# Second cross attention of a two-layer decoder: score products in four quarters of the array, two banks used once, and a new order of steps

## The reference, cut to what matters

```
q = (x @ W_q).reshape(b, n, 8, 64); k, v the same from the context
sim = einsum('bihd,bjhd->bhij', q, k) * 64**-0.5
sim = where(mask, sim, -max)
out = einsum('bhij,bjhd->bihd', softmax(sim), v) @ W_o + b_o
```

## Time and profile before

| | |
|---|---|
| time, median of 3 runs | 274.4 us |
| the three runs | 270.34, 274.4, 275.8 us |
| profiled execution, first to last instruction (span) | 267.4 us |
| TensorE busy | 251.2 us, 94% |
| VectorE, ScalarE, GpSimd busy | 186.4, 146.3, 83.7 us |

### The profile page before, as it was taken

The page is one execution under the profiler, slowest core; times in us unless marked ns, Lnnn a source line. Parts: engine busy times, 40 slices in busy tenths (PEclk is TensorE's granted clock), DMA queues, the critical chain, the costliest instruction groups (busy, mean ns, idle before and its releaser), DMA issues.

```text
span 267.4 us, 5236 instructions
## 1 busy us (share of the span) xinstructions
PE 251.2 (94%) x1842; PEld 174.3 (65%) x1842; DVE 186.4 (70%) x628; ACT 146.3 (55%) x303; POOL 83.7 (31%) x139
## 2 busy tenths in 40 slices
PE   8999899999898999999999768899998999999995
PEld 8663588867665656766675423667986566777775
DVE  4458696799765846476324997668566588889975
ACT  0566665552655587787756335464735944443550
POOL 7733994001010446456765131083331000000000
PEclk9999999999999999999999997999999999999999
DMA  5799900033711000000000000000000000000002
GB/s 143 156 311 251 270 16 2 0 78 101 215 29 53 1 0 0 2 1 0 2 1 1 0 2 0 2 0 2 5 5 0 0 0 4 0 0 2 0 1 81
DMA packets 21991, 11.64 MB, mean 44 GB/s; under 512 B 10968, under 2 KB 20957, under 8 KB 21965
## 3 DMA queue, kind: packets, MB, share of 16 engines
q1 hardware_dynamic: 20925, 10.94, 15.0%
q0 software_dynamic: 80, 0.20, 0.7%
q10 hardware_dynamic: 960, 0.16, 0.3%
HBM read 8.68 MB, written 2.62 MB: 42 GB/s over the span
## 4 chain that ended last, share of the span: by engine, by line
PE 76%; DVE 9%; DMA 5%; ACT 4%; issue 3%; POOL 1%; POOLq 0%; SPq 0%; DVEq 0%
PE bank L1007 10%; PE bank L995 9%; PE bank L884 6%; PE bank L865 5%; PE bank L859 5%; PE bank L764 4%; PE bank L921 3%; PE bank L942 3%; PE bank L743 3%; PE bank L632 3%; PE bank L642 2%; DMA v_scratch<-QKVT 2%; PE bank L667 2%; PE bank L750 2%; PE bank L902 2%
## 5 line engine op out<-in xcount | busy, mean ns | idle before, releaser
L514 POOL TENSOR_TENSOR X<-X,att 128x128 f32<-128x128 f32 x72 | 30.1, 454 | 20.0 <-ACT att L1439 20.0
L440 POOL TENSOR_TENSOR rs<-rs,halves 128x4 f32<-128x4 f32 x14 | 14.3, 1020 | 69.0 <-DVE rs L1696 65.8
L995 PE MATMUL bank<-XT,Wb 128*128 128x512 f32 x64 | 30.0, 600 | 0.7 <-ACT XT L1293 0.7
L1007 PE MATMUL bank<-Wb,att 128*128 128x128 f32 x224 | 27.1, 277 | 0.0
L1007 PEld LDWEIGHTS bank<-Wb,att 128*128 128x128 f32 x224 | 26.1, 192 | 1.4 <-issue 1.4
L1479 ACT ACTIVATE att<-bank 128x512 f32<-128x512 f32 x32 | 18.7, 599 | 8.7 <-PE bank L995 8.5
L1439 ACT ACTIVATE att<-bank,comb 128x128 f32<-128x128 f32 x72 | 20.2, 379 | 4.1 <-PE bank L884 4.1
L1873 DVE SCALAR_TENSOR_TENSOR att<-bank,cols,att 128x512 f32<-128x512 f32 x18 | 13.5, 750 | 11.7 <-ACT att L1428 6.6
L884 PEld LDWEIGHTS bank<-W2a,att 128*128 128x128 f32 x144 | 17.9, 192 | 4.1 <-issue 2.9
L884 PE MATMUL bank<-W2a,att 128*128 128x128 f32 x144 | 18.7, 276 | 0.0
L865 PE MATMUL bank<-XT,W3a 128*128 128x512 f32 x36 | 18.1, 598 | 0.3 <-DVE att L1873 0.3
(11 more groups left out here) (230 smaller groups left out, 513.6 us busy)
## 6 DMA issues: line engine op xcount, KB each, us to landing
Wb<-in_L_ffn_W SPq DMA_DIRECT2D x1, 1024.0 KB, 5.2
Wb<-in_L_ffn_W SPq DMA_DIRECT2D x8, 128.0 KB, 4.8
X<-in_x SPq DMA_DIRECT2D x2, 256.0 KB, 3.2
k_scratch<-QKVT SPq DMA_DIRECT2D x1, 512.0 KB, 3.1
q_scratch<-QKVT SPq DMA_DIRECT2D x1, 512.0 KB, 2.8
Wb<-k_scratch SPq DMA_DIRECT2D x1, 512.0 KB, 4.5
v_scratch<-QKVT SPq DMA_DIRECT2D x1, 512.0 KB, 5.4
V<-q_scratch SPq DMA_DIRECT2D x1, 512.0 KB, 6.2
```

Source lines behind the costliest of these rows:

```text
L440: nc.gpsimd.tensor_tensor(rs[:, 0, cut], rs[:, 1, cut], halves[:, :], ALU.pow).then_inc(l_root[h], 1)
L514: nc.gpsimd.tensor_tensor(X[:, h * HT + t, :], X[:, h * HT + t, :], part0[:, i % 2, t, :], ALU.add).then_inc(f_acc, 1)
L995: mm(bank[i % 4][:, :], W1b[:, e, f * P:(f + 1) * P], XT[:, half(h)], start=True, stop=True).then_inc(m_up, 1)
L1007: last = mm(bank[4 + h][:, t * P:(t + 1) * P], hid[:, e % 2, f, tile], W2b[:, e, f, :], start=(f == 0), stop=(f == F1 - 1))
```

## The change

- `scores1(t)` puts a tile's two batches in two banks, `bank[0]` and `bank[1]`, 256 columns each, for every tile. The rows of the array still come from `h2`, the columns now from `o = h2 ^ b2`: the products go round four quarters, (0,0), (1,1), (0,1), (1,0). There are two mask products of 256 columns for one of 512. Each tile now waits for the subtraction of the tile before (`c_sub >= t`), no longer of the one before that.
- banks 0 and 1 become one tensor, so that `subtract_max1` can read both in one instruction; it orders its output as before. `weigh_values1` picks the transposed probabilities from where `o` put them.
- `add_states` has four steps for five, with the same instructions.
- the lists of steps on all engines get a new order, and some steps a wait that the new order needs (`values0`, `up0_first`, `transpose_xn`, `search_bits`).

```diff
-        bank = [ctx.enter_context(nc.psum_tensor(f"bank{i}", [P, 512], fp32)) for i in range(8)]
+        bank01 = ctx.enter_context(nc.psum_tensor("bank01", [P, 2, 512], fp32))
+        bank = [bank01[:, i, :] for i in range(2)]
+        bank += [ctx.enter_context(nc.psum_tensor(f"bank{i}", [P, 512], fp32)) for i in range(2, 8)]
...
(transpose_xn)
+                if n == 3 and h == 1:
+                    pe.wait_ge(s_gelu[0], 1)
+                if n == 4 and h == 0:
+                    pe.wait_ge(kv_ready, 11)
(values0)
+                pe.wait_ge(ld_x0, 80)
+                pe.wait_ge(prep_act, 2 + h)
(scores1)
-                if t >= 2:
-                    pe.wait_ge(c_sub, t - 1)
-                dst = bank[t % 2]
-                bias = per_col(maskrow[0:1, t * P:(t + 1) * P], NHP)
-                mm(dst[:, :], onesb[0:1, :], bias, start=True, stop=False, skip_group_check=True)
+                if t >= 1:
+                    pe.wait_ge(c_sub, t)
+                for b2 in range(2):
+                    bias = per_col(maskrow[0:1, t * P + b2 * S:t * P + (b2 + 1) * S], NHP)
+                    mm(bank[b2][:, 0:NHP * S], onesb[0:1, :], bias, start=True, stop=False, skip_group_check=True)
                 for hp in range(NHP):
                     for b2 in range(2):
                         for h2 in range(2):
-                            tok = slice(t * P + b2 * S, t * P + (b2 + 1) * S)
-                            last = mm(dst[h2 * S:(h2 + 1) * S, (2 * hp + b2) * S:(2 * hp + b2 + 1) * S],
+                            tok, o = slice(t * P + b2 * S, t * P + (b2 + 1) * S), h2 ^ b2
+                            last = mm(bank[b2][o * S:(o + 1) * S, hp * S:(hp + 1) * S],
                                       Q1T[h2 * DH1:(h2 + 1) * DH1, hp, tok], K1T[h2 * DH1:(h2 + 1) * DH1, hp, tok],
(weigh_values1)
-                                      PTs[b2 * S:(b2 + 1) * S, t % 2, hp * P + h2 * S:hp * P + (h2 + 1) * S],
+                                      PTs[b2 * S:(b2 + 1) * S, t % 2, hp * P + o * S:hp * P + (o + 1) * S],
(subtract_max1)
-                s = bank[t % 2][:, :].rearrange("p (a s) -> p a s", s=S)
-                then(V.tensor_reduce(sm[:, t, 0, :], s, AX.X, ALU.max))
+                s = bank01[:, :, 0:NHP * S].rearrange("p b (a s) -> p a b s", s=S)
+                peak = sm[:, t, 0, :].rearrange("p (a b) -> p a b", b=2)
+                then(V.tensor_reduce(peak, s, AX.X, ALU.max))
(search_bits)
+                dve.wait_ge(c_pv, NT - 1)
```

More of the change, by code:

```diff
@@ L579, in _ @@
             add_part(1, 2, 1)
+            root(3, 0)
             add_part(1, 2, 2)
@@ L1068, in _ @@
             scores(3)
+            transpose_probs(0)
             transpose_values(0)
@@ L1071, in _ @@
             transpose_values(2)
-            transpose_probs(0)
-            scores(4)
             transpose_probs(1)
             transpose_values(3)
+            weigh_values(0)
+            scores(4)
+            transpose_probs(2)
             scores(5)
             scores(6)
-            transpose_probs(2)
-            weigh_values(0)
             power(1)
+            transpose_probs(3)
             weigh_values(1)
-            transpose_probs(3)
             weigh_values(2)
@@ L1085, in _ @@
             power(2)
+            weigh_values(3)
+            transpose_probs(5)
+            power(3)
             scores(7)
-            weigh_values(3)
-            power(3)
-            transpose_probs(5)
+            power(4)
             weigh_values(4)
+            scores(8)
             transpose_probs(6)
-            power(4)
-            scores(8)
             weigh_values(5)
@@ L1239, in _ @@
             transpose_probs1(2)
+            scores1(5)
             weigh_values1(1)
-            scores1(5)
             project_out(0)
+            transpose_probs1(3)
             scores1(6)
-            transpose_probs1(3)
             weigh_values1(2)
@@ L1561, in _ @@
             cross0_q(1)
+            weigh0(0, 1)
             silu(0, 4)
@@ L1655, in _ @@
             gelu(0, 1, 1)
+            copy_ys(0, 0)
             for e in range(E1):
@@ L2124, in _ @@
             add_states(0, 3)
-            add_states(0, 4)
             ln_moments(4, 0)
             states_moments(1)
+            states_scale(1)
             ln_apply(4, 0)
-            states_scale(1)
             states_apply(1)
@@ L2165, in _ @@
             ln_apply(5, 1)
-            search_bits()
             route()
```

116 lines of the change are left out of this document (57 added, 59 removed).

## The result

The changed kernel takes 279.14 us in the median of 4 runs (274.53 to 282.0); the kernel before took 272.37 in its 4 runs beside them. The ratio is 1.0225, with a 95% interval from 1.0141 to 1.0308: slower, by 1.4 to 3.1%. The ratios and intervals of this text take only the runs that lie within 1.5% of the fastest of the same kernel, while its medians and its means of lost time take all of them, so the two can differ. The forecast was 274.0 us and a range up to 277.0. It was wrong, and on the slow side.

What follows compares the result with a forecast made beforehand. TensorE, busy 251.2 of 267.4 us, was taken to bound the kernel, with VectorE setting the pace in two places. Terms -1.4 + 0 + 1.0 + 0 = -0.4 gave span 267.0 and time 274.0 us, range 269.5 to 277.0.

Steps and rivals of the forecast that it cites:

- The step that failed: Before the second cross attention's first scores: the clock fall at 160 to 164 us comes again, 1.6 us lost.
- The sum: All terms: -1.4 second cross attention, 0 at 26 us, +1.0 first attention, 0 for the rest; -0.4 us in all.
- Rival B: At 167 to 171 us: clock falls a second time if the wait before scores1(1) reaches 1.4; 276.0 us, chance 0.14.
- my own other wait of a microsecond, at 72 us: First attention: transpose_probs(15), already waiting 0.78 us at 72.25 for copy_probs(14), goes to 73.25.
- The products in four quarters: Second cross attention's score products: 0.62 us a tile for 1.08, so 0.46 gained each, 3.7 us for eight tiles.
- Rival C: Score products: placing doesn't matter, passes stay at 34 ns while the second bank is gone; 277.2 us, chance 0.09.
- Single buffering and the opening: Second cross attention: waits of 1.4 before scores1(1), 0.85 before scores1(5); opening 0.35 late, net gain taken as 1.4 us.
- The 1.75 "given back to waits": Opening of the second cross attention: loss to waits that double buffering hid, against 1.4 us won in three tiles.
- The gap at 26 us: First attention: wait before scores(2) goes, TensorE idles 1.7 before weigh_values(0); between -1.45 and +0.3, taken as 0.
- The gap at 64 us: First attention: subtract_max(14) behind ln_apply(1, 0) leaves VectorE idle 1.2 us, later steps late; +1.0, bounds 0 and +1.4.
- The 274.4: Starting time of the kernel before, median of three runs, 7.0 us above its profiled span of 267.4.

Runs made afterwards that it cites:

- e8: The kernel before, unchanged, run for a second profile: 270.51 us.
- e18: Repeat of e17 (e1 with 6 unused products before scores1(1) and 1 before scores1(2)): 271.75 us, ratio 1.0079.
- e3: Changed kernel with the score products in two quarters of the array again, two banks and single buffering kept: 281.5 us, ratio 1.0432.
- e12: Kernel before with the new lists of steps up to 70 us alone: 276.66 us.
- e16: e12 with 5 unused products right before transpose_probs(15): 272.01 us, ratio 1.0074.
- e4: Changed kernel with subtract_max(14) back ahead of ln_apply(1, 0) on VectorE: 277.04 us, ratio 1.0263.
- e15: e14 with 22 unused products in TensorE's waits: 265.74 us, ratio 0.9835 to the kernel before.
- e14: Kernel before up to 165 us, then the change's score products and order, second tile's scores in banks 3 and 4: 268.55 us, ratio 0.9943.
- e7: Changed kernel with 67 unused products in TensorE's waits: 276.0 us, ratio 1.0203 to the kernel before.
- e11: Changed kernel with 30 unused products, at the same places as e7: 270.57 us, ratio 1.0043 to the kernel before.
- e1: Kernel before with the change's score part alone (four quarters, two banks, single buffered), all lists in the old order: 277.8 us, ratio 1.0208.
- e17: e1 with 6 unused products right before scores1(1) and 1 before scores1(2): 273.92 us, ratio 1.0103 to the kernel before.
- the two halves of the change: Kernel before with the score part alone in the old order: 277.8 us; changed kernel's order alone, with the score part of before: 277.98 us.
- e10: Changed kernel with the second tile's scores in banks 3 and 4: 276.72 us, ratio 1.0217 to the kernel before.

## Why the prediction was wrong

**The step that failed** is the one on the clock: "the same thinness is there after the change, so I expect the fall again: 1.6 us lost". One fall, at the place and of the size that the profile of before happened to have, was carried over, and every other wait was priced at its own length. That fall did not even come: in the profile of the changed kernel the granted clock is 1.00 from 160 to 173, and the way from the transposes of the fourth normalisation to scores1(0), forecast at 7.9 us with a fall in it, is 6.75 us (167.21 to 173.96) against 8.44 before (158.39 to 166.83). Falls came at 26, 77 and 176 instead. The sum has no term for a change in what the clock takes, and measured it is 6.9 us (10.3 lost against 3.4). The page of before could have warned: the runs there spread over 5.5 us while the profiled one had a single fall of 1.6. I called that scatter; e8 and the 81 runs show that it is mostly the clock.

**Rival B** named the mechanism and the place: "it decides if the wait before scores1(1) is 1.4 us or more". The wait was 1.75, the clock fell at 176.6, and e18 shows, for the old order, that filling such a wait takes the fall away. It was sized at one fall of 1.7; it was two such, 3.4 us in this profile, and it had a chance of 0.14 for want of a second look at my own other wait of a microsecond, at 72 us. The argument "against", that 148 to 154 was as thin and the clock held, is no argument: in e8 the fall came at 154 to 158, right behind it.

**The products in four quarters:** right. 0.62 us a tile measured, and e3 shows that the placing does it. Rival C is out. (Its size didn't follow from its own terms either: a gain of 1.4 without the 3.7 is a loss of 2.3, not 1.4 to 2.2.) In the changed kernel the placing is worth 2.2 us of the 3.7 at full clock (e3 against it); that waits for the subtraction take the rest is likely, but was not measured.

**Single buffering and the opening:** the waits were sized nearly right, 1.75 and 0.95 for 1.4 and 0.85. From scores1(0) to the transposes of the fifth normalisation the changed kernel takes 35.0 us (173.96 to 208.95) and the kernel before 33.7 (166.83 to 200.57), but 3.4 of the 35.0 are clock, so at full clock the part is 2.1 us shorter. The forecast has 1.7 for this: its start 0.6 late and its end 1.1 early. (The 1.75 "given back to waits" hold that late start; the waits in the opening were 1.15 of it.) What was priced too low is the way there: from the transposes of the second normalisation (80.34, after: 87.48) to those of the fourth (158.39, after: 167.21) the changed kernel takes 79.7 us and the one before 78.05, of which the forecast had 1.2 for ln_apply(4, 0) behind states_scale(1). The other 0.5 was not followed up. And by the transposes of the second normalisation the changed kernel is 7.1 us late: 5.1 of these are the two falls, 1.0 was forecast, and most of the rest is the late load of Q that follows here.

**The gap at 26 us:** the trade was as laid out, and its wait, forecast at 1.7, is 1.69 or 1.70 in eight of the nine profiles with the new early order. In the profile shown it is 1.20, and two things stand ahead of it there. The load of Q from DRAM landed later, which has no part in the change, and the copy that widens Q held TensorE for 2.19 us; then came the fall at 26. In e12 the load was as late (7.6 us in both), TensorE waited 2.40 us, the clock held, and the wait is 1.69: so it is the slow clock that ate into the wait, and a wait of 2.40 us can pass without a fall.

**The gap at 64 us:** forecast +1.0. VectorE's idle time is as forecast (1.23 for 1.2). From the transposes of the first normalisation to the second, e16, in which the clock held there, takes 15.05 us (66.37 to 81.42) against 14.32 before (66.02 to 80.34): 0.7, its unused products lying inside the wait. e4, which undoes the step, agrees as far as its runs can tell (0.9). Its larger price was behind it: the 0.38 us that it added to the wait before transpose_probs(15) makes a fall there likely (five profiles of five, against two of eight), and filling that wait is worth 4.7 us (e12 against e16).

**The sum.** At full clock the changed kernel is 1.1 us slower than before, forecast -0.4. That error of 1.5 would have stayed inside the range. The 6.9 of the clock did not. The starting point was off too, and hid part of the miss. The distance of 7.0 us between span and median isn't a property of the kernel: every run lists a span 1.7 to 1.8 us below its time, and the rest is longer spans. The 274.4 came from three runs, two of them high, of a kernel whose median over 81 runs is 270.4. From there the same sum gives 270.0, 9 us below the measured 279.14 and not 5.

## What to carry to other kernels

Before pricing a new order, run the old kernel several times and work out span x clock and span x (1 - clock) of each: if the second scatters, the kernel sits at the edge, and a wait of TensorE between thin products can cost, beside its length, the half speed of the dense products behind it. Ask of each wait that a change makes longer what TensorE would be doing in it; a few unused products in the wait, sized by their measured time, are a quick test of whether the clock is the loss, and here they are a gain too (e15 against e14: 265.7 against 268.6); too many cost more than the clock gives back (e7 against e11: 276.0 against 270.6). And here a second buffer was needed most at the first tiles, where no other work lies between; there a bank that is only used later will do.

## What the runs showed of the hardware

- Score products of 64x64, two passes each, take 19 ns a pass if they go round four quarters of the array and 34 if they go to two, with row halves alternating in both (e3 against the changed kernel).
- An unused 128x128 product in fp32 (two passes), in a row of such, takes about 0.26 us: 10 passes in 1.28 us, 12 in 1.60.
- A fall of the clock costs in portions: the lost time of the kernel before was within 0.3 us of 0, 1.6, 3.5, 5.1, 6.8 or 8.5 us in every one of the 81 runs.
- The load of Q from DRAM (512 KB in small pieces) took 6.1 to 6.3 us to land in most profiles and 7.2 to 7.6 in five, in the old order (e1, e14, e17) and in the new (the changed kernel, e12) alike.
- A wait of TensorE makes a fall of the clock more likely and doesn't settle it: of the profiles with 1.16 us idle before transpose_probs(15) five of five have a fall that begins there, with 0.78 two of eight, with the wait filled none of six.
- Why the two halves of the change don't add up in lost time (9.9 and 9.6 alone, 10.3 together), and why a fall moves when one place is mended (e4, e10), stays open; no run was made for it.
